# A Mamba, mixture-of-experts and linear-attention kernel: GpSimd weighs three of the 16 states of a forward unit in place of two

## The reference, cut to what matters

```
x = conv(x) + conv_b ; x = silu(x)                    # 512 channels
x_dbl = x @ Wx.T                                      # gives dt (64), B (16), C (16)
dt = softplus(x_dbl[..., :64] @ Wdt.T + bdt)
deltaA = exp(dt * A)                                  # 16 states per channel
dBu = dt * B * x
def step(carry, inp):
    carry = dA_t * carry + dBu_t
    y_t = einsum('bdn,bn->bd', carry, C_t)            # weigh each state by C and add up
y = ys + x * D
return y * silu(z)
...
s = (out_forward + out_backward[:, ::-1]) / 2 @ W_out.T
```

## Time and profile before

| | |
|---|---|
| median of three runs | 3044.89 us |
| the profiled execution | 3049.27 us, span 3047.5 us |
| DVE busy over the span | 73% |
| PE busy over the span | 90% |
| POOL busy over the span | 57% |
| first layer, the 16 units | 85 to 1983 us of the span |
| a forward unit (of the third batch on) | about 122.1 us |
| a backward unit | about 114.9 us |

### The profile page before, as it was taken

One profiled execution on the slowest core, in us unless ns is written; L12 is line 12 of the kernel. 1 busy time (PEld: TensorE's weight loads), 2 busy tenths in 40 slices (PEclk: granted clock), 3 DMA queues, 4 the chain that ended last, 5 costly groups with the idle time before them and its releaser, 6 DMA issues. The chain is left out here.

```text
span 3047.5 us, 37649 instructions
## 1 busy us (share of the span) xinstructions
PE 2727.6 (90%) x13924; PEld 1733.8 (57%) x13924; DVE 2231.5 (73%) x2586; ACT 1778.6 (58%) x2734; POOL 1729.4 (57%) x565
## 2 busy tenths in 40 slices
PE   5577998999899899899899898778999999999999
PEld 2243665666666666666565665654645556555564
DVE  8899999999999999999999999954334243342420
ACT  4556688698688688688777877513233232332322
POOL 2899888888888888888979979821011010110000
PEclk9788999999999999999999999988999999999999
DMA  7222333243334333433333333340001010010000
GB/s 275 77 73 76 127 128 123 99 155 112 111 127 143 114 122 118 143 112 128 114 112 130 132 119 111 112 163 28 1 34 34 0 34 7 28 34 0 7 7 7
DMA packets 143594, 272.72 MB, mean 89 GB/s; under 512 B 23032, under 2 KB 94175, under 8 KB 142431
## 3 DMA queue, kind: packets, MB, share of 16 engines
q1 hardware_dynamic: 137310, 254.12, 24.3%
q0 software_dynamic: 6144, 16.79, 1.6%
HBM read 230.75 MB, written 40.11 MB: 89 GB/s over the span
## 5 line engine op out<-in xcount | busy, mean ns | idle before, releaser
L1051 POOL TENSOR_TENSOR hs<-u,bb 128x2048 f32<-128x2048 f32 x254 | 1151.0, 4539 | 206.6 <-PE hT L1277 194.5
L1192 DVE TENSOR_TENSOR_SCAN hs<-dA,hs 128x1024 f32<-128x1024 f32 x512 | 1166.6, 2285 | 71.2 <-ACT dA L1097 50.8
L1097 ACT ACTIVATE dA<-dt,cols 128x511 f32<-128x511 f32 x1024 | 658.9, 680 | 258.6 <-DVE hs L1192 253.8
L1277 PE MATMUL hT<-ident,hs 128*128 128x128 f32 x3648 | 527.3, 285 | 179.1 <-DVE held L1204 136.8
L1204 DVE SCALAR_TENSOR_TENSOR held<-hT,ct,held 128x512 f32<-128x512 f32 x880 | 613.3, 741 | 20.8 <-PE hT L1277 20.3
L1277 PEld LDWEIGHTS hT<-ident,hs 128*128 128x128 f32 x3648 | 417.6, 145 | 332.5 <-DVE held L1204 124.6
L1559 ACT ACTIVATE gl<-bank,cols_sb 128x512 f32<-128x512 f32 x192 | 130.6, 687 | 527.3 <-PE bank L1798 527.1
L1798 PE MATMUL bank<-mT,cms_sb 128*128 128x512 f32 x768 | 362.8, 597 | 10.1 <-ACT mT L1553 8.6
L144 POOL COPY cur<-slot 128x8 uint32 (+1 forms) x8 | 1.5, 188 | 637.1 <-DVE held L156 628.9
L1301 PEld LDWEIGHTS moe<-xgT,held 128*128 128x128 f32 x2272 | 280.7, 196 | 71.0 <-issue 65.0
L1301 PE MATMUL moe<-xgT,held 128*128 128x128 f32 x2272 | 283.6, 279 | 0.3
(11 more groups left out here) (233 smaller groups left out, 3515.7 us busy)
## 6 DMA issues: line engine op xcount, KB each, us to landing
held<-wl SPq DMA_DIRECT2D x71, 1024.0 KB
bb<-b_scratch SPq DMA_DIRECT2D x128, 512.0 KB, 4.7
held<-wl SPq DMA_DIRECT2D x71, 512.0 KB
xg<-xg_scratch SPq DMA_DIRECT2D x71, 128.0 KB
yg_scratch<-yg SPq DMA_DIRECT2D x71, 128.0 KB, 1.7
held<-x SPq DMA_DIRECT2D x16, 512.0 KB, 6.8
xg_scratch<-zero SPq DMA_DIRECT2D x8, 1024.0 KB, 7.0
cb<-b_scratch SPq DMA_DIRECT2D x28, 256.0 KB, 5.8
```

Of the source, the lines that this page charges most:

```text
L1051: nc.gpsimd.tensor_tensor(hs[n % HS][:, :, :], u[d][:, :, :], row, ALU.mult).then_inc(dBu_ready, 1)
L1097: last = nc.scalar.activation(dst, src, ACT.Exp, scale=cols[:, at:at + 1])
L1192: nc.vector.tensor_tensor_scan(h, decay, h, 0.0, ALU.mult, ALU.add).then_inc(scan_done, 1)
L1277: last = nc.tensor.transpose(hT[c % 2][:, k * P:(k + 1) * P], hs[n % HS][:, k, c * P:(c + 1) * P], ident[:, :])
```

## The change

States 2, 6 and 9 of a forward unit are weighed by GpSimd in place of 2 and 9; backward units keep 2 and 9. The counts of semaphores follow. Along with it go new entries in the tables: `add_skip` of a backward unit stands behind S7 and not S9, the second `soft` of a forward unit stands one state later, VectorE weighs the second half of the first state one slot earlier, the piece `c` moves by one or two slots, ScalarE's decay stands behind the pieces in other slots, and TensorE's spare products stand in other slots: 17 in a forward unit in place of 19, and 17 in a backward one in place of 12.

```diff
-        POOLN = (2, 9)
-        NP, NW = len(POOLN), NS - len(POOLN)
+        POOLN = ((2, 6, 9), (2, 9))
+        NP = [len(at) for at in POOLN]
-        N_ADD = 2 * NP + 1
-        SKIP_AT = 9
+        N_ADD = sum(NP) + 1
+        SKIP_AT = 7
-        BEHIND, TURNED = (1, 2, 3, 4), (0, 1, 2, 3)
+        BEHIND, TURNED = (1, 1, 3, 4), (0, 1, 2, 3)
...
-            return NW * unit + 2 * NP + n - sum(m < n for m in POOLN)
+            return NS * unit - pooled(unit) + n - sum(m < n for m in by_pool(unit))
+        def pooled(unit):
+            return sum(NP) * (unit // 2 - 1) + NP[0] * (unit % 2)
...
-        plan(0, "c", (16,))
+        plan(0, "c", (15,))
-        plan(1, "c", (16,))
+        plan(1, "c", (18,))
-        SOFT = ((13, 13, 15, 15), (14, 14, 15, 15))
+        SOFT = ((13, 14, 15, 15), (14, 14, 15, 15))
-        LATE = ((3, 14, 16, 17, 18, 21, 22, 24, 25, 27, 29, 30), (3, 5, 14, 16, 18, 19, 20, 27, 28, 29, 30, 31))
+        LATE = ((3, 9, 10, 12, 14, 17, 18, 21, 22, 24, 25, 27, 29, 30), (3, 14, 18, 19, 20, 23, 24, 27, 28, 29, 31))
-        WEIGH, ADD = ((1, 2), (2, 2)), ((3, 3), (3, 3))
+        WEIGH, ADD = ((1, 2, 2), (2, 2)), ((3, 2, 3), (3, 3))
-        SPARE = ({10: 1, 13: 1, 15: 1, 17: 1, 20: 4, 25: 4, 26: 1, 27: 1, 28: 1, 29: 3, 31: 1}, {0: 1, 19: 1, 24: 2, 26: 3, 27: 2, 29: 1, 31: 2})
+        SPARE = ({10: 1, 14: 1, 15: 1, 16: 2, 17: 1, 20: 2, 25: 1, 26: 1, 27: 1, 28: 2, 29: 1, 30: 2, 31: 1}, {0: 1, 4: 1, 19: 1, 20: 1, 21: 1, 22: 2, 24: 2, 25: 1, 26: 2, 27: 2, 29: 1, 31: 2})
...
-                            for k, m in enumerate(POOLN):
-                                if n == m + 2 and (k < NP - 1 or more) and (not in_first_batch(unit) or d == 1 and k == NP - 1):
+                            for k, m in enumerate(POOLN[d]):
+                                ends = k == NP[d] - 1
+                                if n == m + 2 and (not ends or more) and (not in_first_batch(unit) or d == 1 and ends):
                                     if not in_first_batch(unit):
-                                        sp.wait_ge(p_mul, NP * (unit - 2) + k + 1)
-                                    load_c(d if k < NP - 1 else 1 - d, POOLN[(k + 1) % NP])
+                                        sp.wait_ge(p_mul, pooled(unit) + k + 1)
+                                    load_c(1 - d if ends else d, POOLN[1 - d][0] if ends else POOLN[d][k + 1])
```

More of the change, by code:

```diff
@@ L270, in turned @@
                 return NS * unit + n
-            return NW * unit + 2 * NP + n - sum(m < n for m in POOLN)
+            return NS * unit - pooled(unit) + n - sum(m < n for m in by_pool(unit))
+        def pooled(unit):
+            return sum(NP) * (unit // 2 - 1) + NP[0] * (unit % 2)
         def by_pool(unit):
-            return () if in_first_batch(unit) else POOLN
+            return () if in_first_batch(unit) else POOLN[unit % 2]
         PREP = [{s: [] for s in range(2 * NS)} for _ in range(2)]
@@ L406, in prepare_copies @@
                     if d == 1:
-                        act.wait_ge(p_add, N_ADD * b - 2 * NP)
+                        act.wait_ge(p_add, N_ADD * b - sum(NP))
                     elif later(b):
-                        act.wait_ge(p_add, N_ADD * b - NP)
+                        act.wait_ge(p_add, N_ADD * b - NP[1])
                 nc.scalar.activation(xc[d][:, k, :], src[:, :], ACT.Identity,
@@ L1005, in adds @@
                 def adds(d, b, k):
-                    return N_ADD * b + NP * d + k - 2 * NP + (1 if d == 1 and POOLN[k] + ADD[d][k] > SKIP_AT else 0)
+                    return N_ADD * b - sum(NP) + NP[0] * d + k + (1 if d == 1 and POOLN[1][k] + ADD[1][k] > SKIP_AT else 0)
                 def weigh(d, unit, k):
-                    m = POOLN[k]
+                    m = POOLN[d][k]
                     pool.wait_ge(scan_done, 2 * (NS * unit + m) + 4)
-                    pool.wait_ge(cb_in, 16 * (NP * (unit - 2) + k + 1))
+                    pool.wait_ge(cb_in, 16 * (pooled(unit) + k + 1))
                     row = cb[:, :].rearrange("p (a l) -> p a l", a=1).broadcast_to([P, DB, L])
@@ L1016, in add @@
                 def add(d, unit, b, k):
-                    m = POOLN[k]
-                    pool.wait_ge(p_mul, NP * (unit - 2) + k + 1)
+                    m = POOLN[d][k]
+                    pool.wait_ge(p_mul, pooled(unit) + k + 1)
                     other = ysum
@@ L1029, in add_skip @@
                     pool.wait_ge(skip_ready, DB * unit + DB)
-                    done = sum(m + a <= SKIP_AT for m, a in zip(POOLN, ADD[1]))
+                    done = sum(m + a <= SKIP_AT for m, a in zip(POOLN[1], ADD[1]))
                     if not in_first_batch(unit):
-                        pool.wait_ge(p_add, N_ADD * b - NP + done)
+                        pool.wait_ge(p_add, N_ADD * b - NP[1] + done)
                     nc.gpsimd.tensor_tensor(ysum[:, :, :], ysum[:, :, :], xc[1][:, :, :], ALU.add).then_inc(p_add, 1)
@@ L1040, in state @@
                     if n >= HS and n - HS in by_pool(unit):
-                        pool.wait_ge(p_add, adds(d, b, POOLN.index(n - HS)) + 1)
+                        pool.wait_ge(p_add, adds(d, b, POOLN[d].index(n - HS)) + 1)
                     elif n >= HS:
@@ L1339, in body @@
                         if d == 1:
-                            pe.wait_ge(hT_used, 4 * (NW * (unit + 1) + 2 * NP) + 2)
-                            pe.wait_ge(p_add, N_ADD * (b + 1) - 2 * NP)
+                            pe.wait_ge(hT_used, NC * turned(unit, NS) + 2)
+                            pe.wait_ge(p_add, N_ADD * (b + 1) - sum(NP))
                             for k in range(DB):
```

## The result

The changed kernel takes 3057.46 us (median of six runs, 3057.12 to 3063.53), the kernel before 3044.89 us in the same comparison. The ratio is 1.0044, with a 95% interval from 1.0032 to 1.0057. That is 12.6 us more, slower by over 0.2%, and inside the range, near its upper end.

The account below looks back on a forecast made before the run. VectorE paces a forward unit up to S11, GpSimd from there to the end. Terms of 0.2 + 0.4 + 0.1 + 0.2 = 0.9 us per forward unit, 6.3 in 7, gave 3051.2, put at 3050 us for overlap; range 3038 to 3060.

Parts of the forecast that it names:

- What bounds a unit: Forward unit: VectorE paces up to S11, GpSimd after; 9.17 us of new work into 8.64 us of gaps costs 0.2 us.
- the slack of 0.3 us at the unit's end: Forward unit's hand-over: the next unit's S0 ends 0.3 to 0.4 us before its scan, absorbing part of GpSimd's delay.
- The start of the unit: Forward unit: weighing state 0's chunks earlier delays a turning, a tile and S8 by 0.4 us, bounds 0 and 0.5.
- S11: GpSimd piece in forward units needing state 7 turned, level with GpSimd's own time: cost 0.1 us, bounds 0 and 0.5.
- The row of C: Load for state 9, now behind `store_b`, lands about when W9 is due: 0.2 us per forward unit, bounds 0 to 0.4.
- The rival built on it: The row of C lands 1.3 to 1.8 us after W9's time, adding 9 us: 3060 us, chance 0.15.
- The sum of the forward units: 0.2 + 0.4 + 0.1 + 0.2 = 0.9 us per forward unit, 6.3 us in 7.
- The waits of VectorE: In forward units VectorE waits about 3 us for S9 at state 9's scan, and again at the next unit's first scan.
- The backward units: Moved `add_skip`, new LATE and five more spare products cost 0, bounds -0.5 and +0.5 us per unit.
- The rival that the gain comes through: VectorE's saved 2.8 us per forward unit shorten it: fully 19.5 us, 3025 us; a third of it, 3037; chance 0.13.
- that outcome: GpSimd without gaps: moving the elementwise work there makes a forward unit 6.4 us longer, 45 us in all; given no chance.
- "Slower": Whole kernel slower by over 0.2%: the late-row rival's 0.15 plus half of the forecast, 0.26, together 0.41.

Follow-up runs that it names:

- pool_only: Kernel before plus only the third pooled state (state 6 on GpSimd) and its semaphore counts, all other tables as before: 3053.10 us, ratio 1.0022.
- behind_back: Changed kernel with the table BEHIND as before, so state 0's last two chunks are weighed behind the scan of state 3: 3054.88 us, ratio 1.0023.
- row_early: Changed kernel with the load of the row of C ahead of `store_b` again: 3060.22 us where the kernel before took 3052.8, ratio 1.0022.
- no_add6_late: Changed kernel without the add of state 6 (missing from the output) and with ScalarE's order LATE as before: 3053.22 us, ratio 1.0023.
- no_work6: pool_only without GpSimd's weighing and add of state 6 (missing from the output): 3054.42 us where the kernel before took 3052.8, ratio 1.0007.
- pool_add_late: pool_only with the add of state 6 one state later, behind S9: 3057.41 us, ratio 1.0036.

## Why the prediction was right, and where it was not

**What bounds a unit.** Right in the main reading: not the sum of GpSimd's idle time but the 8.64 us of it behind S8 decided, and a unit moves with the start of S11. After the change there is no gap behind S8, GpSimd is busy for 108.0 us and VectorE for 110.7 (forecast 109 and 110.6), and pool_only prices the overfull gaps by themselves at 0.3 us per unit (forecast 0.2).

The 0.2 came of two errors that nearly cancel. S11 starts 0.3 us later in pool_only, where the prediction's chain had it 0.4 later. And the slack of 0.3 us at the unit's end, which was to swallow part of it, was not there: the scan of state 14 starts when S14 ends, and from there VectorE has no gap to the end. That scan in the kernel before, and in unit 10 of the changed kernel:

```profile
1144.40 2.29 DVE L1192 TENSOR_TENSOR_SCAN hs<-dA,hs 128x1024 f32<-128x1024 f32 x1 [0.77 <-POOL hs L1051]
...
1389.55 2.29 DVE L1197 TENSOR_TENSOR_SCAN hs<-dA,hs 128x1024 f32<-128x1024 f32 x1 [0.33 <-ACT dA L1102]
```

In the changed kernel the moved `soft` brings S14 early (it ends 2.4 us ahead of that scan), and a decay is late instead. So VectorE, held by decays, and GpSimd now reach the end of a unit nearly together: S0 ends 0.34 us ahead of its scan in unit 10, and 0.10 us, that is at once, in units 2 and 8. (The prediction counts ten pieces of work from S11 to the next S0; there are eleven, four of them of half size. Nothing hangs on it.)

**The start of the unit.** Right: 0.4 forecast, 0.5 measured by behind_back in the units without another delay.

**S11.** Forecast 0.1. Measured: nothing. GpSimd has no gap ahead of S11, so S11 doesn't wait for the turning of state 7.

**The row of C.** Its price was put at 0.2 us per unit. Measured: 0.36 and 0.23 us in two of seven units, and row_early gives 0.25 us back over all seven. It was within its bounds of 0 to 0.4 but counted too high. The rival built on it did not happen in the changed kernel, but shows wherever GpSimd is early (behind_back, no_add6_late).

**The sum of the forward units.** 6.3 us forecast, 6.2 measured. Part of that agreement is luck. The measured parts are 0.3 + 0.5, two terms were counted too high, and the rest is a term that the prediction did not have: late `bb` rows at S8, which cost nothing before and now go through (unit 6 of the changed kernel, 1.24 us late, was 123.3 us long).

**The waits of VectorE.** One right, one wrong. The scan of state 9 waits 3.1 us for S9, as forecast (3). The second wait, at the next unit's first scan, is not there: VectorE waits 1.67, 0.27 and 0.33 us for decays on the way, and both engines arrive together. I had counted VectorE's slack twice, since the wait for S9 had already used it.

**The backward units.** The step that failed: "I take 0, bounds -0.5 and +0.5 per unit". Measured: +0.65 per unit between the two profiled executions, 3.9 us in all. This is beyond the 0.5 us that the prediction itself had named as a sign of being wrong. I weighed the new spare products against TensorE's 14 us of idle time, the sum over the unit, which is the very reading I had warned of for GpSimd. What counts is that in all six of these units the stretch at the clock's lower level falls at 100 us, where a turning is needed at once. The clock was not among my terms. That the new products cause the whole of it is not shown: over all traces they go with 0.15 us per unit, and pool_only loses 0.46 per unit with its backward units unchanged.

**The rival that the gain comes through.** It had 0.13, for the wrong reason. I gave it to the case that GpSimd's chain starts earlier. no_work6 shows that with GpSimd's extra work gone altogether, the forward units would give 7 x 0.4 = 2.8 us at best and not 19.5: the other chains of TensorE and ScalarE lie that close behind. The Trainium skill (GPSIMD Engine Reference, "Engine selection") argues that such work belongs on VectorE, and from its own rows the prediction put that outcome at 6.4 us per unit. The trace shows 0.3 for the pooled state alone: the page's direction was right, and the gaps set the size.

**The forecast's place.** 3050 us against 3057.46, 7.5 us short. The forward units account for 1.1 of it, since I had taken 1.2 off their sum for overlap. The backward units are 3.9, and the start and the last unit 0.5. The profiled stretch behind the last scan went the other way by 2.2, and 4.2 come from how far each profiled execution lay from its median. "Slower" had 0.41 and "the same" 0.46. The forward units alone lie at the edge of both, and terms that the forecast did not have carried the time on to the upper end of its range.

**Open.** Why the lower stretch lies at 92 us in most units with the old spare products and at 100 us in others with the same tables; how much of the backward loss the change causes; how pool_add_late's loss divides; where row_early's lower ratio comes from; and the stretch behind the last scan (1059 to 1066 us over the 14 traces) and 0.8 us ahead of the first scan, which no edit reaches.

## What to carry to other kernels

An engine's idle time is worth what its gaps can take at the place where the new work must stand, and gaps that look free also absorb late transfers: filling them costs more than their sum says. Before work is moved off a busy engine, leave it out altogether in one kernel: here that showed a second chain 0.4 us behind the first, which caps the gain whatever the work costs elsewhere. One trace per kernel is a thin base for a difference of a few us: here units that no edit touched moved by 2.75 us in all, and only a table over all traces showed it. Read idle time by place for every engine that a change touches, also for the edit that seems to be free.

## What the runs showed of the hardware

I had not expected how much the place of one short stretch of TensorE at the 1.2 GHz level decides. A stretch of 3.4 us cost a backward unit nothing at 92 us (nor did one of 6.8 us at 90 us, but for one unit of 13), and 0.4 to 0.9 us at 100 us. Together with one at 82 to 86 us, a stretch of 3.4 or 6.8 us at 99 to 106 us cost 2.1 to 2.6 us. The mean clock doesn't show it: it is 0.99 in the window of 114.90 us before and in the one of 115.74 us after.
